# The count stage of a graph kernel: half of each block's last cast goes from ScalarE to VectorE

## What is computed

```python
edge_index = jnp.stack([src, dst])
x = _layernorm(x + _L0_gnn_ref(x, edge_index, ...))          # two layers of h = x @ W; segment_sum(h[src], dst)
x = _layernorm(x + _L1_gnn_ref(x, src, dst, edge_weight1, ...))   # edge network, summed over the edges of a node
x = _layernorm(x + _L2_gnn_ref(x, node_vec1, edge_index, edge_weight, ...))
x = _layernorm(x + _L3_gnn_ref(x, L3_gnn_W, L3_gnn_bias, edge_index, 3125))   # polynomial of the graph's Laplacian
```

## Time and profile before

| | us |
|---|---|
| median of 3 runs | 1568.72 (1567.54 to 1569.63) |
| the profiled execution | 1570.59 |
| its span | 1568.0 |
| count stage, first ACT cast to last DVE copy | 191.6 to 332.4 |

### The profile page before, as it was taken

The page is one execution under the profiler, slowest core; times in us unless marked ns, Lnnn a source line. Parts: engine busy times, 40 slices in busy tenths (PEclk is TensorE's granted clock), DMA queues, the critical chain, the costliest instruction groups (busy, mean ns, idle before and its releaser), DMA issues. The chain is left out here.

```text
span 1568.0 us, 43052 instructions
## 1 busy us (share of the span) xinstructions
PE 1395.5 (89%) x16795; PEld 1289.7 (82%) x16795; DVE 1209.8 (77%) x3560; ACT 627.8 (40%) x1180; POOL 43.2 (3%) x82
## 2 busy tenths in 40 slices
PE   1845488789988999999999969899999999999997
PEld 0534466679986888888888849799999999999997
DVE  6899888855557888888888867677677677677676
ACT  0279799941116777777777742500000000000000
POOL 2111000000000000000000010000000000000000
PEclk9979799989999999999999979899999999999999
DMA  1000055430015454453332160000000000000000
GB/s 28 2 0 0 6 152 157 141 103 22 2 43 138 138 154 117 136 155 98 97 95 77 59 162 1 6 2 1 2 2 1 2 2 2 2 2 2 2 7 18
DMA packets 36900, 83.82 MB, mean 53 GB/s; under 512 B 22829, under 2 KB 23861, under 8 KB 36767
## 3 DMA queue, kind: packets, MB, share of 16 engines
q1 hardware_dynamic: 33633, 81.46, 18.3%
q10 hardware_dynamic: 2880, 0.37, 0.2%
q0 software_dynamic: 256, 0.15, 0.1%
HBM read 60.76 MB, written 21.14 MB: 52 GB/s over the span
## 5 line engine op out<-in xcount | busy, mean ns | idle before, releaser
L1966 PE MATMUL L_psA<-second,mat 125*128 125x192 bf16 x3125 | 259.0, 246 | 0.0
L1966 PE MATMUL L_psA<-L_parts,mat 125*128 125x192 bf16 x3125 | 258.6, 246 | 0.0
L1966 PEld LDWEIGHTS L_psA<-second,mat 125*128 125x128 bf16 x3125 | 257.6, 98 | 0.6
L1966 PEld LDWEIGHTS L_psA<-L_parts,mat 125*128 125x128 bf16 x3125 | 258.0, 98 | 0.1
L1915 ACT COPY L_wk<-L_Wk 128x64 f32<-128x64 f32 x8 | 1.6, 242 | 378.7 <-PE L_psA L1966 378.7
L1264 PEld LDWEIGHTS L_ps_pre<-L_drow,mat 128*128 128x128 bf16 x2250 | 128.3, 98 | 30.0 <-issue 0.6
L2019 DVE TENSOR_REDUCE L_sumr<-L_psA 125x64 f32<-125x192 f32 x225 | 80.4, 357 | 71.3 <-PE L_psA L1966 71.1
L1264 PE MATMUL L_ps_pre<-L_drow,mat 128*128 128x32 bf16 (+3 forms) x2250 | 132.7, 212 | 0.0
L684 PE MATMUL ps_count<-onehot 128*128 128x125 bf16 x1200 | 106.8, 218 | 15.3 <-DVE onehot L647 7.7
L1453 DVE TENSOR_TENSOR L_e<-L_e,mat 128x512 f32<-128x512 f32 x125 | 86.1, 689 | 40.5 <-ACT L_e L1351 40.5
L647 DVE TENSOR_TENSOR onehot<-iota_bf,codes 128x1024 bf16<-128x1024 bf16 x150 | 100.6, 686 | 19.3 <-PE ps_count L684 18.1
(11 more groups left out here) (326 smaller groups left out, 2402.3 us busy)
## 6 DMA issues: line engine op xcount, KB each, us to landing
L_drow<-rows_d SPq DMA_DIRECT2D x25, 728.0 KB
mat<-m_d SPq DMA_DIRECT2D x25, 684.2 KB
mat<-rows_d SPq DMA_DIRECT2D x25, 640.0 KB, 4.2
m_d<-panel SPq DMA_DIRECT2D x13, 684.2 KB
m_d<-xb SPq DMA_DIRECT2D x12, 684.2 KB
L_drow<-rows_d SPq DMA_DIRECT2D x25, 84.5 KB
mat<-m_d SPq DMA_DIRECT2D x25, 79.4 KB
m_d<-panel SPq DMA_DIRECT2D x13, 79.4 KB
```

Source lines behind the costliest of these rows:

```text
L1966: last = nc.tensor.matmul(ps[:, 0:3 * D], t.mat[0:B, kb, b * B:b * B + P], parts[src][:, kb].rearrange("p r d -> p (r d)"), start=(kb == 0 ...
```

## The change

The sixth part (n = 5) of a block was moved by one ACT cast of both banks. Now ACT casts bank h = 0 alone (125x500, tiles 16 to 19) and raises `moved` as before. Bank h = 1 (tiles 20 to 23) is cast by DVE in a new step `move_half(b)`, which waits for the block's sixth count and raises a new semaphore `half_moved`. DVE does it in the next block, between its wait before group 2 and group 2 itself; for the last block behind the loop. PE waits for `half_moved` in addition before part n = 2 of every block but the first.

```diff
+                def move_half(b):
+
+                    dve.wait_ge(counted, EV * b + 6)
+                    nc.vector.tensor_copy(t.mat[0:B, 20:24, bass.ds(b * B, B)], ring[2][0:B, 1, 0:4 * B].rearrange(
+                        "p (c n) -> p c n", n=B)).then_inc(half_moved, 1)
+
...
                         elif g in (0, 2) and not (isinstance(b, int) and b == 0):
                             dve.wait_ge(counted, EV * b - 3 if g == 0 else EV * b - 1)
+                        if g == 2 and not (isinstance(b, int) and b == 0):
+                            move_half(b - 1)
                         one_hots(k, g)
...
                 in_pairs(dve, NB, body, last=2)
+                move_half(NB - 1)
                 move_last(NB - 1, 0)
...
                             if i == 0:
                                 room(b, 2 * u)
+                                if u == 1 and b:
+                                    pe.wait_ge(half_moved, b)
...
-                        nc.scalar.copy(t.mat[0:B, tiles[0]:tiles[-1] + 1, bass.ds(b * B, B)].rearrange(
-                            "p (h c) n -> p h c n", h=2), in_ring(2 * u + 1)).then_inc(moved, 1)
+                        n = 2 if u < NU - 1 else 1
+                        nc.scalar.copy(t.mat[0:B, tiles[0]:tiles[0] + 4 * n, bass.ds(b * B, B)].rearrange(
+                            "p (h c) n -> p h c n", h=n), in_ring(2 * u + 1)[:, 0:n]).then_inc(moved, 1)
```

More of the change, by code:

```diff
@@ L599, in count_matrices @@
         stored = l0.panel_stored
-        padded, staged, hot_ready, counted, moved, last_moved, wdone, rows_out = map(sem, (
-            "padded", "codes_staged", "onehots_ready", "counted", "blocks_moved", "last_moved", "w_summed",
+        padded, staged, hot_ready, counted, moved, half_moved, last_moved, wdone, rows_out = map(sem, (
+            "padded", "codes_staged", "onehots_ready", "counted", "blocks_moved", "half_moved", "last_moved", "w_summed",
             "rows_out"))
```

## The result

| | before | the change |
|---|---|---|
| median, us | 1569.18 | 1578.84 |
| lowest to highest, us | 1567.54 to 1570.64 | 1577.87 to 1580.17 |
| profiled execution, us (its span) | 1570.59 (1568.0) | 1578.55 (1576.4) |

The change is slower by 9.7 us: the ratio is 1.0061, with a 95% interval of 1.0049 to 1.0073. That is the case to which the prediction gave 0.42, slower by over 0.2%, and its direction was the forecast's; but the time is outside the range, which ended at 1574.4 us.

The account below looks back on a forecast made before the run. It took a two-block loop through ACT, PE, DVE and the panel's store as the bound. Cast +3.1, registers +0.4, end -0.4 gave +3.1 us on the median 1568.72, so 1571.8 us; range 1568.2 to 1574.4.

Parts of the forecast that it names:

- The loop through the store: ACT's first casts, PE, DVE, `move_last`, panel store, ACT two blocks on: said to set the pace, 11.06 us per two blocks.
- ACT's 0.42 us: ACT's sixth cast, halved, is 0.42 us cheaper: worth nothing per pair, -0.4 us once at the stage's end.
- B: Step from ACT's third cast's end to DVE's next instruction behind PE's part 5; forecast 0.92 us unchanged, apart from register work.
- Rival B: DVE's new cast is dear, 0.75 to 0.90 us start to start: 1573.7 to 1575.5 us; chance 0.12.
- The cover in front of group 4: DVE's idle time between groups 3 and 4, mean 0.33 us, absorbs part of the new cast, leaving 0.26 net.
- C: Step from DVE's next instruction behind PE's part 5 to `move_last`'s first cast; forecast 0.26 us longer.
- Register work behind the wait: Two ISA instructions on DVE between wait and new cast: 0.03 us, between 0 and 0.1; x12 = 0.4 us.
- Step 2 of the loop: From the end of ACT's cast n=2, via PE's part n=5, to DVE's start: 0.92 us, put down as unchanged.
- PE's added wait: PE's wait for `half_moved` at part n=2: already met, since DVE finishes the half before group 2; costs nothing.
- Rival A: The store isn't last before ACT's even-block first cast: pair 10.76 us, -4.0 us in all, 1564.7 us; chance 0.10.
- E: Step from SP's issue of the panel store to ACT's first cast two blocks on; forecast used 4.29 us.
- Rival C: Only some pairs are closed by the store; elsewhere ACT's 0.42 pays: 1568.2 to 1570.0 us; chance 0.18.

Follow-up runs that it names:

- the relief alone: The change without DVE's new cast and `half_moved`; the uncast tiles are zeroed once by GpSimd: 1582.80 us, ratio 1.0083, its stage beginning 11.8 us late.
- the early store: SP stores all but the last 128 columns after the block's fifth move, the rest after `move_last`: 1565.68 us in the kernel before, 1559.26 in the change.
- the cast alone: The change with ACT not relieved: DVE casts bank 1, then ACT still casts both banks, waiting for `half_moved`: 1575.44 us, ratio 1.0039.
- filled: The change plus 12 PE matmuls per block whose result nobody reads: 1577.00 us, ratio 1.0053; again 1576.87 us, ratio 1.0057.
- written out: The change with DVE's loop unrolled to constant addresses: 1578.11 us, ratio 1.0057; with 12 unread PE matmuls per block as well, 1574.97 us, ratio 1.0035.

## Why the prediction missed

Point by point, in its order:

- **The loop through the store bounds the kernel.** Right. ACT's saved time appears as DMA waits in front of even blocks, the kernel with the relief alone repeats the old 10.9 us pairs, and the early store turns the sign of the change.
- **ACT's 0.42 us are worth nothing per pair, and 0.4 once at the end.** The second is right: from block 24's first cast to the last `move_last` there were 331.71 - 326.14 = 5.57 us, and now 339.95 - 334.79 = 5.16. The first is right at full clock and wrong in the mean: the relief has a cost, because the clock goes down with it, 0.22 to 0.26 us of B (the change beside the cast alone, the relief alone beside before). With the store early, where ACT goes on without a wait, the half cast is followed after 0.49 (270.42 to 270.91) in place of 0.89: it saves 0.40, for the 0.42 forecast.
- **The cast takes 0.59 to 0.60 us.** Right, 0.59 (219.78 to 220.37). The recorded duration is 0.68, the number that the prediction worked out by the Trainium skill's rule (VectorE: DVE Perf Modes, section The DRAIN you can't avoid), but the next instruction starts before that has passed; the trace disagrees with the rule, as the rows of before did. The same section adds that an operation that isn't held back starts earlier, and that is how the trace has it. Rival B, which needed 0.65 or more, fell.
- **The cover in front of group 4 holds 0.33 of it.** Right: C grew by 0.25 in the mean, the forecast's net was 0.26.
- **Register work behind the wait, 0.03.** This is the first step that failed: it is 0.18 on DVE, and another 0.07 stands between wait and cast that the register work doesn't explain. The price was taken from SP's single register operation, the nearest row but on another engine, and even the upper bound of 0.1 was well under what there was. Over the stage, in the eleven pairs that the loop serves, the register work makes 2.0 us, and the 0.07 in all twelve 0.8.
- **Step 2 of the loop, 0.92 us, unchanged.** This is the second, and the larger one. The prediction took the full clock of the earlier trace rows as given. It asked of every engine what the change would make it do, but not of PE in how long pieces it would idle. B's growth beyond the two terms above is 3.2 us over the stage, all of it in the seven blocks at a lower clock.
- **PE's added wait is met already.** In the loop, yes. But PE does wait for DVE's later one-hots now (total, times, longest, from 200 to 330 us), of which the table of before lists none:

```profile
PE ps_count L693 <- DVE onehot L653: 10.4, 28, 0.5
```

  The row of 252.06 is one of them. They are not on the path by themselves, and they don't make the clock fall by themselves: the kernel with the cast alone has pauses of 0.35 to 0.45 us at the same place and keeps the full clock.
- **Rival A (the store isn't last)** fell with the DMA waits of 16.2 us, E stayed at 4.46 in the mean, 4.24 at the least in the even blocks of both kernels. **Rival C (the loop is tight only in part)** fell too: no even block gained; every one of the twelve pairs is longer than before.
- **A slip in Rival A, of no weight.** The profile's KB are of 1024 bytes, so the store is 782,000 bytes; the fit that the prediction takes from the Trainium skill (DMA: Bandwidth & Descriptors, section Anatomy of one DMA) then gives 3.79 us and not 3.75, an estimate, and the rival's time by it 1565.8 and not 1565.3.

In sum the forecast was 3.1 us: cast 3.1, registers 0.4, end -0.4. The stage shows cast 3.0, registers 2.0, the other 0.07 behind the wait 0.8, slower stretches of PE 3.2, E -0.4, and -0.4 at the end: 8.2 us, of which the profile has 8.5 - 0.4 = 8.1. The loop, the cast and its cover were right; the miss lies in B, which grew by 6.0 us over the stage where the forecast had 0.4. The spans of the two profiled executions differ by 8.4 us and their times by 8.0; the medians differ by 9.7, because the profiled execution of before was 1.4 over its median.

**What stays open.** The clock's share of the total. In the stage it is shown three times (relief alone; cast alone beside the change; filled beside not filled), as 2.8 to 4.1 us of length in each, 2.3 to 3.2 of it in B. In the medians the last two showed 2.6, 1.8, 1.2 and, written out, 3.1 us, against 2 to 7 us from the lowest run of a kernel to its highest, and what follows behind the last `move_last` took between 1233.5 and 1237.6 us in these profiles, for no reason that they show. That pauses in fewer and longer pieces are what lets the clock fall is argued and not shown: no run changed the pauses and nothing else, and the length of one pause doesn't tell whether a fall follows (0.45 and 0.74 us without, 0.40 and 0.75 with, 1.08 without in the kernel before). Open is also why E, mostly 4.2 to 4.8 us, is 5 to 6 in one or two blocks of most profiles, the kernel before (5.14 in block 6) included.

## What to carry to other kernels

Before work is moved off the busiest engine, close the loop that sets the pace, in rows, and see whether the moved work lies inside or outside it; here ACT was 95% busy and its relief worth nothing, and a store issued two microseconds earlier was what made the relief pay. Work that is put behind the wait of a loop costs its register instructions too, so put it in front of a wait that ends late anyway. And when TensorE waits in the loop, look at the granted clock of the stretch, not only at busy shares: relieving another engine lowered it here, by the way in which TensorE's idle time is dealt out, as far as the profiles tell.

## What the runs showed of the hardware

- The register work of two ISA instructions between a wait and a cast on DVE cost 0.18 us after the wait was met (cast 0.29 behind PE's last matmul in a loop, 0.11 with constant addresses).
- TensorE's granted clock fell to 0.50 within a stage in which PE was busy 80% of the time (115.1 of 143 us), behind pauses of 0.40 and 0.75 us close together; nearly equal pauses in another block went without a fall. The Trainium skill (TensorE: Matmul & The Clock Gate, section HAM oscillation) describes a clock that falls where PE stands still for a DMA; the pauses here are much shorter than the DMA waits of its example.
- Four GpSimd memsets, 10.6 us in all, ran beside two DVE casts of 128x104 from SBUF, and the casts took 10.55 and 10.47 us, that is until the memsets were through, where they take 0.20 to 0.21 in the kernel before.
- ACT casts that never wait are recorded with 1.67 us instead of 0.99 to 1.1, and still start 0.89 apart: the duration on the record is no price, the distance between starts is.
